# Score rows by halves of a tile in two attentions, and reciprocals spread as 16-bit halves

## The reference

```python
x = x + L0_attn(layernorm(x))   # 16 heads of 16, window |i-j| <= 128, then a projection Wp
x = x + L0_ffn(layernorm(x))    # 8 experts, the best 2 per token, and one shared
x = x + L1_attn(layernorm(x))   # 16 heads of 16, blocks of 64 tokens
x = x + L1_ffn(layernorm(x))    # product with ternary weights
```

## Time and profile before

| | |
|---|---|
| median of three runs | 2438.78 us (2435.6 to 2440.25) |
| profiled execution | 2437.45 us, its span 2435.7 us |
| mean granted TensorE clock | 0.947 of 2.4 GHz |
| first attention | about 173 to 694 us |
| combine | about 698 to 790 us |
| second attention | about 1672 to 2300 us |
| TensorE, VectorE, ScalarE, GpSimd busy | 90%, 76%, 68%, 44% |

### The profile page before, as it was taken

How to read it: one execution, slowest core, us unless ns; L and a number is a source line. 1 busy time by engine, 2 the same in 40 slices (tenths; PEclk the granted TensorE clock), 3 DMA queues, 4 the chain that set the end, 5 groups by cost and what they waited for, 6 DMA issues and landing times. The chain is left out here.

```text
span 2435.7 us, 73430 instructions
## 1 busy us (share of the span) xinstructions
PE 2200.0 (90%) x25549; PEld 1344.8 (55%) x25549; DVE 1840.5 (76%) x5599; ACT 1661.7 (68%) x3892; POOL 1072.9 (44%) x1370
## 2 busy tenths in 40 slices
PE   7979999999969688879999995996999999999765
PEld 4643444444436576768888884563444444444354
DVE  5539999999829577755445444984999999999298
ACT  7955888889942555525445443893699999999644
POOL 3533666666654466646666664562000000000076
PEclk9987999999979899989999998997899999999888
DMA  6552333333232567646654344884232232322242
GB/s 231 199 183 72 91 91 92 92 90 92 67 89 77 138 189 187 163 129 125 144 127 106 92 92 118 270 274 149 63 80 74 78 79 78 79 75 68 65 152 96
DMA packets 363698, 289.65 MB, mean 119 GB/s; under 512 B 228401, under 2 KB 296753, under 8 KB 363345
## 3 DMA queue, kind: packets, MB, share of 16 engines
q1 hardware_dynamic: 349616, 248.24, 37.2%
q0 software_dynamic: 12960, 35.60, 4.5%
q10 hardware_dynamic: 768, 1.12, 0.2%
HBM read 133.53 MB, written 123.69 MB: 106 GB/s over the span
## 5 line engine op out<-in xcount | busy, mean ns | idle before, releaser
L740 ACT ACTIVATE a_pr<-a_pst 128x384 f32<-128x384 f32 (+3 forms) x2176 | 908.8, 486 | 117.0 <-PE a_pst L775 79.7
L775 PE MATMUL a_psc<-a_ke,a_qe 52*128 52x128 f16 (+5 forms) x3072 | 648.6, 291 | 32.7 <-DMA a_ke<-mrow 29.2
L692 DVE TENSOR_REDUCE a_mx<-a_psc 128x1 f32<-128x384 f32 (+2 forms) x1152 | 566.9, 564 | 18.9 <-PE a_psc L775 13.7
L775 PE MATMUL a_pst<-a_qe,a_ke 53*128 53x128 f16 (+5 forms) x3072 | 564.3, 281 | 2.7 <-ACT a_pr L740 0.4
L836 PE MATMUL a_po<-a_pr,a_ve 128*17 128x128 f32 (+3 forms) x10496 | 562.1, 302 | 2.0 <-ACT a_pr L740 1.2
L687 DVE CUSTOM_DVE_ANT_0 a_cut<-a_psc,row_mask 128x384 bf16<-128x384 f32 (+1 forms) x1024 | 472.7, 521 | 23.4 <-PE a_psc L775 11.5
L775 PEld LDWEIGHTS a_pst<-a_qe,a_ke 53*128 53x128 f16 (+1 forms) x3072 | 210.3, 94 | 330.1 <-ACT a_pr L740 187.5
L658 POOL TENSOR_SCALAR_AFFINE_SELECT a_pr<-a_pr 128x512 f32<-128x512 f32 x448 | 275.1, 634 | 163.2 <-ACT a_pr L740 163.2
L775 PEld LDWEIGHTS a_psc<-a_ke,a_qe 52*128 52x128 f16 (+1 forms) x3072 | 223.5, 94 | 143.7 <-DVE a_mx L692 44.5
L836 PEld LDWEIGHTS a_po<-a_pr,a_ve 128*17 128x17 f32 x10496 | 193.9, 96 | 191.2 <-issue 116.3
L638 POOL TENSOR_SCALAR a_mneg<-a_mx 128x32 f16<-128x32 f32 x64 | 18.4, 288 | 632.5 <-DVE a_mx L696 588.1
(11 more groups left out here) (234 smaller groups left out, 4172.7 us busy)
## 6 DMA issues: line engine op xcount, KB each, us to landing
a_qe<-qx SPq DMA_DIRECT2D x378, 64.0 KB, 2.6
a_ke<-kx SPq DMA_DIRECT2D x378, 64.0 KB, 2.7
vx<-p_vst SPq DMA_DIRECT2D x32, 544.0 KB, 3.4
a_ve<-vx SPq DMA_DIRECT2D x64, 272.0 KB, 3.1
qx<-p_stg SPq DMA_DIRECT2D x64, 256.0 KB, 3.4
kx<-p_stg SPq DMA_DIRECT2D x64, 256.0 KB, 3.3
ox<-a_ost SPq DMA_DIRECT2D x256, 64.0 KB
x_res<-x SPq DMA_DIRECT2D x16, 512.0 KB, 8.9
```

Of the source, the lines that this page charges most:

```text
L692: dve.tensor_reduce(out.unsqueeze(1), psc[(u * n_s + n) % RING][:, 0:width], AXX, ALU.max)\
L740: act.activation(pr[s % SLOTS][:, h // 2, h % 2, 0:width], pst[prob_slot(u, n) % RING][:, 0:width], ACT.Exp, scale=scale).then_inc(p_ready, 1)
L775: last = pe.matmul(out[:, col:col + count], stat, mov(tok, count), start=(k == 0), stop=(k == len(pieces) - 1), skip_group_check=True, til ...
```

## The change

Score tiles are made per half of 64 tokens. `window_rows` and `band_rows` give the runs of columns of a half: for inner tiles of the window the 320 columns that its 64 tokens can reach, for inner tiles of the block attention 128 columns of tile 0 and the 192 columns of three blocks. The maxima are taken over 320 columns in place of 384 for these tiles (six of eight jobs in the window, five of nine in the block attention); `row_mask` gets a fourth part of 320 columns, whose lower 64 rows have another layout than the upper ones. Edge tiles and the two wide jobs of tile 0 keep their columns. The probability tiles keep theirs too, but go through the same `product`, which now issues two matmuls per run of columns: stationary columns 0 to 63 at tile position (64 * par, 0) and 64 to 127 at (64 * par, 64).

In `Shares`, the reciprocals are split into two fp16 parts, a copy scaled by 4096 on ScalarE and the rest on VectorE, and spread by two fp16 matmuls in place of one fp32 product. `stage_constants` makes the new mask: three more selects on GpSimd, then a copy and a memset on VectorE and one select on GpSimd.

```diff
+def window_rows(t, half):
+    if 0 < t < TB - 1:
+        return [(t * P - P + 64 * half, 320, 0)]
+    return [(0 if t == 0 else N - 2 * P, 2 * P, 0)]
+
+def band_rows(t, half):
+    at = t * P - 64 + 64 * half if 1 < t < TB - 1 else P if t == 1 else N - 192
+    return [(0, P, 0), (at, 192, P)]
...
+        wide = (0,) if len(jobs) > TB else ()
+        def score_runs(j, half):
+            return jobs[j][1] if jobs[j][0] in wide else row_runs(jobs[j][0], half)
+        row_width = [sum(r[1] for r in score_runs(j, 0)) for j in range(nj)]
...
-                    width = sum(p[1] for p in pieces)
+                    width = row_width[j]
...
-                        at = 0 if t > 0 else P
+                        at = (3 * P if t < TB - 1 else 0) if t > 0 else P
...
-            def product(par, out, stat, mov, pieces, ready):
-                for k, (tok, count, col) in enumerate(pieces):
-                    last = pe.matmul(out[:, col:col + count], stat, mov(tok, count), start=(k == 0),
-                                     stop=(k == len(pieces) - 1), skip_group_check=True, tile_position=(64 * par, 0))
+            def product(par, out, t, stat, mov, runs, ready):
+                for k in range(len(runs[0])):
+                    for half in range(2):
+                        tok, count, col = runs[half][k]
+                        at = slice(64 * half, 64 * half + 64)
+                        last = pe.matmul(out[at, col:col + count], stat[:, t * P + 64 * half:t * P + 64 * half + 64],
+                                         mov[:, tok:tok + count], start=(k == 0), stop=(k == len(runs[0]) - 1),
+                                         skip_group_check=True, tile_position=(64 * par, 64 * half))
                 last.then_inc(ready, 1)
...
-                product(par, psc[(u * n_s + n) % RING], qe[g][rows(par, KS), i, t * P:(t + 1) * P],
-                        lambda tok, count: ke[g][rows(par, KS), i, tok:tok + count], pieces, s_ready)
+                product(par, psc[(u * n_s + n) % RING], t, qe[g][rows(par, KS), i, :], ke[g][rows(par, KS), i, :],
+                        [score_runs(j, half) for half in range(2)], s_ready)
...
-                product(par, pst[k % RING], ke[g][rows(par, KR), i, t * P:(t + 1) * P],
-                        lambda tok, count: qe[g][rows(par, KR), i, tok:tok + count], pieces, t_ready)
+                product(par, pst[k % RING], t, ke[g][rows(par, KR), i, :], qe[g][rows(par, KR), i, :],
+                        [pieces, pieces], t_ready)
...
+    def high(self, act, half):
+        cols = slice(half * CH, half * CH + CH)
+        act.wait_ge(self.ready, half + 1)
+        act.activation(self.rec_hi[:, cols], self.rec[:, cols], ACT.Copy, scale=SHS).then_inc(self.high_done, 1)
+
+    def low(self, dve, half):
+        cols = slice(half * CH, half * CH + CH)
+        dve.wait_ge(self.high_done, half + 1)
+        dve.scalar_tensor_tensor(out=self.rec_lo[:, cols], in0=self.rec[:, cols], scalar=SHS, in1=self.rec_hi[:, cols],
+                                 op0=ALU.mult, op1=ALU.subtract).then_inc(self.low_done, 1)
...
-        return pe.matmul(out, self.spread[:, at:at + P], self.rec[:, (c % 2) * CH:(c % 2) * CH + CH],
-                         start=True, stop=True)
+        pe.matmul(out, self.spread[:, at:at + P], self.rec_hi[:, cols], start=True, stop=False)
+        return pe.matmul(out, self.spread[:, at:at + P], self.rec_lo[:, cols], start=False, stop=True)
...
+            for half in range(2):
+                shares.high(act, half)
             act.wait_ge(s_w, 16)
...
             for c in range(2):
                 shares.invert(dve, c)
+                shares.low(dve, c)
                 share(c)
...
+            band = row_mask[:, 3 * P:3 * P + 320]
+            dve.wait_ge(s_cut, 7)
+            dve.tensor_copy(band[64:P, 256:320], band[64:P, 64:128]).then_inc(s_set, 1)
+            dve.wait_ge(s_set, 5)
+            dve.memset(band[:, 64:128], 0.0).then_inc(s_set, 1)
+            dve.wait_ge(s_set, 6)
...
+            band = row_mask[:, 3 * P:3 * P + 320]
+            for at, sign, base in ((0, 1, 64), (256, -1, 0), (64, -1, -64)):
+                pool.affine_select(out=band[:, at:at + 64], in_=band[:, at:at + 64], compare_op=ALU.is_ge, fill=NEG, base=base,
+                                   pattern=[[sign, 64]], channel_multiplier=-sign).then_inc(s_cut, 1)
+            pool.wait_ge(s_cut, 7)
+            pool.affine_select(out=band[0:64, 0:64], in_=band[0:64, 0:64], compare_op=ALU.is_ge, fill=NEG, base=0,
+                               pattern=[[1, 64]], channel_multiplier=-1).then_inc(s_cut, 1)
+            pool.wait_ge(s_cut, 8)
```

23 lines of the change are left out of this document (14 added, 9 removed).

## The result

The changed kernel takes **2424.81 us** (median of 7 runs, 2421.17 to 2429.95) against 2438.95 (7 runs, 2435.6 to 2442.2) for the kernel before on the same chip: ratio 0.9937, 95% interval 0.9925 to 0.995. It is faster by 14 us, not by the 46 us of the forecast. Of the rivals, E ("nothing arrives in the coupled parts", 2429 us) stands nearest. The time lies inside the stated range of 2345 to 2460 us, because the range was wide enough to hold E, not because the forecast's mechanism came true. The profiled execution took 2425.1 us, its span is 2423.4 us.

A forecast was written before the change was run, and what follows sets the result against it. VectorE was taken to bound both attentions, TensorE 0.12 us a wide step behind. Gains of 27 (first attention), 15 (second) and 6 (combine) less 2 (constants) made 46 us: 2438.8 to 2393 us, range 2345 to 2460.

The forecast's parts named there:

- E: Both attentions: three banks each of scores and probabilities tie engines into one loop, no gain in coupled parts; 2429 us, chance 0.13.
- TensorE takes over from VectorE: Both attentions: wide steps fall from VectorE's 1.90 us towards TensorE's 1.76; the forecast case, 2393 us, chance 0.60.
- The same 0.7: First attention: 0.7 us a unit lost in hand-overs, on top of the slowest engines' sum, before and after.
- stays below: First attention: ScalarE, 1.52 us a wide step plus two output copies of 0.60 us in one step, doesn't bind.
- 15 ns a half step: Both attentions, TensorE: assumed cost of issuing the halved products, against 27 ns gained by narrower scores.
- D: Both attentions: a product's second half waits for the first in the same rows; 2629 us, chance 0.12.
- C: Both attentions: each extra pair of load and matmul costs TensorE 25 ns of issue; 2499 us, chance 0.08.
- Second attention, 12 us: Second attention, later units: five 384-column steps fall from 1.90 to 1.81 us, 0.4 us a unit over 30 units.
- First two units: Start of each attention, scores and maxima alone: VectorE's saving counts in full, 3.2 and 2.6 us.
- Combine: Combine stage: fp16 spreading makes VectorE the bound, 3.8 us a chunk; start effects cancel; 6 us gained, from 2 to 8.
- Constants: Before the first load of x: added memset, selects and a hop count in full; 2 us lost, from 1 to 3.
- The rule against the change: TensorE's split products: a skill rule implying halves in the same row group can't overlap; outweighed by V's eight loads in 0.13 us.

The follow-up runs named there:

- narrow alone: Kernel before with undivided products and maxima over only the first 320 of 384 columns: 2425.42 against 2445.71 us, ratio 0.9921.
- light maxima: Changed kernel with every maximum over 128 columns, the other columns left out: 2398.05 us, ratio 0.9802.
- both readers light: Changed attentions with the combine stage of before, exponentials over 256 of 384 columns and maxima over 128: 2389.8 us, ratio 0.9762.
- lighter exponentials: Changed attentions with the combine stage of before, exponentials over 256 of 384 columns: 2421.87 against 2443.9 us, ratio 0.9911.

## Why the prediction was off, point by point

- **"TensorE takes over from VectorE"**: the step that failed. The forecast let a wide step of the first attention fall from VectorE's 1.90 us to TensorE's 1.76, with nothing in between. In between stood the loop through one bank of scores, 1.94 us a step before, with one maximum in it in place of four: a step saves 0.066 us and not up to 0.26. Six wide steps: 0.40 us a unit; narrow alone gave 0.34. The forecast had 0.8. VectorE's pace itself was read rightly (1.91 us by the starts), and TensorE's too (1.75 us in undisturbed steps with light maxima). That VectorE was busy 97% and that its step nearly equalled the measured one was taken as proof that nothing else held the step.
- **"The same 0.7" of hand-overs**: there was no constant loss on top of the slowest engine. The hand-overs (0.59 us from a product's start to its maximum, 0.065 back) are in the loop itself: 0.65 of the 1.21 us for which a bank is held. With both readers light, the medians of the steps add up to 13.9 us, TensorE's bare 13.8 and hardly more.
- **ScalarE "stays below", with both copies in one step**: the copies lie in two steps, the third and the eighth. Before, these take 1.94 and 1.95 us (medians), with narrow maxima alone 1.94 and 1.95 as well, with light maxima 1.98 and 2.00, and only with light exponentials on top 1.85 and 1.81. The third is one of the six wide steps that were to fall to 1.76.
- **Issue of the halves, "15 ns a half step"**: the halves do start together (the records of a product 2 to 4 ns apart, so D is out; products unhindered take 0.44 us as before, so C is out). But the product's result reaches VectorE 24 ns later (0.586 to 0.610), and in the second attention 33 ns (0.409 to 0.442 where VectorE waits for it, the shortest tenth). This stands in the loop, against a gain of 66. What is left is 44 ns a turn, 0.26 us a unit by six steps; measured over the inner tiles, 0.970 to 0.948 a half step, the same 0.26. The narrow steps at the ends of a unit gave 0.09 back, which leaves 0.17.
- **Second attention, 12 us**: here VectorE did bind before: a maximum began 0.525 us after its product, where 0.409 is enough. Its relief ran into the next limit at once. It came to 0.1 us over the inner tiles (0.915 to 0.904 a half step) and 0.02 over the unit; narrow alone gave 0.17. Only 40% of the banks are still taken at once. The fifth and sixth step show the limit (medians): 1.86 and 1.89 us before, 1.88 after, 1.88 also with maxima over 128 columns, 1.82 with lighter exponentials, 1.78 with both, near TensorE's forecast 1.76. So the exponentials hold these steps, while the forecast put ScalarE below TensorE; by which wait they do wasn't isolated.
- **First two units**, 3.2 and 2.6 us: 2.5 and 2.5. Right in kind and near in size: nothing but scores and maxima runs there.
- **Combine**, 6 us: right in kind, too small. The first product came 1.4 us later after the stage's start (7.0 to 8.4), as forecast. From chunk to chunk it was 4.34 us before and is 3.82 now by VectorE's products, as the forecast's 3.8 had it; TensorE, which runs ahead, starts its chunks 3.48 us apart in the middle and 3.82 at the end. Twelve chunks give 6.2 us of the 9.2. The forecast let the start of the stage cancel out, and there most of the rest was gained: the second chunk follows the first after 7.4 us in place of 7.9, the third the second after 3.3 in place of 5.4, as the four records of a chunk are 0.4 us apart in place of 3.75 us for four. VectorE after, its products with the spread reciprocals of two chunks:

```profile
729.79 1.27 DVE L1069 SCALAR_TENSOR_TENSOR c_att<-c_ot,c_pb 128x512 f32<-128x512 f32 x2
...
733.61 1.27 DVE L1069 SCALAR_TENSOR_TENSOR c_att<-c_ot,c_pb 128x512 f32<-128x512 f32 x2
```

- **Constants**, 2 us: 1.6. Right.
- **Rival E** had the mechanism (three banks tie the engines into one loop) and the very row, 401.38, that shows it. I gave it 0.13 because "wide steps follow VectorE's 1.90 closely", without adding up the loop from the rows that I had: 0.59 and 0.56 and 0.06, then 0.27 and 0.45 to 0.56, are 1.93 to 2.04 us. That sum was to be had before.
- **The rule against the change** (the Trainium skill, "TensorE: Matmul & The Clock Gate", Part 3: a weight load overlaps products in flight only if its row group differs) was weighed rightly: halves that share rows start together in every profile with both products halved, so for tiles beside each other in the columns it doesn't hold here.

Still open: why the turned maxima land late once VectorE is light. Their DMA waits (0.8 us a unit with light maxima, 1.1 with both readers light) and the lower clock after the longer ones stand behind the distance between 15.2 us a unit and the 14.4 and 13.9 of the medians; how much each is worth wasn't separated. A fourth bank of scores beside three of probabilities wasn't tried, since no bank is left.

## What to carry to other kernels

When engines hand tiles round in few buffers, follow one buffer from the instruction that fills it to the next one that does, add up that turn, and count how often the instruction you shorten stands in it; the saving per turn is that, whatever the engine's share of busy time. A gap of the same 60 ns between the reader's end and the next writer, on most tiles, shows the turn that binds, even where a list of waits has little; but make sure that the reader isn't full itself, since that leaves the same gap. Then ask for the limit behind it: here a step could fall by 0.07 us in the first attention and by next to nothing in the second. And when a run leaves work out, look at the granted clock and at medians of steps, before its mean is read as a limit. Before splitting an instruction on such a turn, price the later arrival of its result, not only its issue.

## What the runs showed of the hardware

- A maximum starts 0.54 to 0.61 us after its product starts (320 or 384 columns, fp16), and where the bank binds, the next product on it starts 62 to 67 ns after the maximum's record ends.
- The split product's result comes 24 to 33 ns later than the whole one's, though both halves start within 4 ns; 6144 more pairs of load and product over the full array cost 5 us in the whole kernel.
- Products over the full 128 columns between products of 64 columns run one after the other, 0.40 to 0.43 us apart at 1.2 GHz.
- With half the V products the first attention stayed at 1.2 GHz and got slower, by 3 us a unit. With light maxima, each of three waits of TensorE of 2.2 us and more for a DMA was followed by 10 to 14 us at 1.2 GHz.
- Loads of 128 KB in place of two of 64 made the loads queued behind them land later, 7.9 us for 3.0.
